# Down products of a shared expert: from row chunk by row chunk to feature tile by feature tile

## The chip, the cores and the metric

The kernel runs on one core of a Trainium2 chip. The metric is the time of one execution on the device in microseconds (us), as the median of several runs. The traces show one execution each, with the engines TensorE (PE; its weight loads are PEld), VectorE (DVE), ScalarE (ACT), GpSimd (POOL) and SyncE (SP, which only issues DMAs here).

## The reference

Input is x of 2 x 2048 rows by 256 features. It is layer-normalised to xn. The output is x + attention(xn) + moe(xn):

```python
xn = layernorm(x)
# attention: 16 heads of 128, blocks with decay, silu on q, k, v, rms norm, sigmoid gate, output product
# moe: 64 experts, top 4 by router logits, plus 2 shared experts that every row passes:
sg = silu(einsum('nd,sdh->nsh', xn, swg))      # S=2, h=256: 512 gate features
su = einsum('nd,sdh->nsh', xn, swu)            # 512 up features
shared = einsum('nsh,shd->nd', sg * su, swd)   # down product, 512 -> 256
```

The change touches the last line only, in the order of its work.

## The kernel before

The kernel has two phases. The **first phase** takes the 4096 rows in NSB = 8 groups of 512 rows (SB), each of CH = 4 row chunks of 128 rows. For each group it normalises the rows, turns them (features onto partitions), computes the router's logits and the choice of experts, and does the whole shared expert. The **second phase** takes 128 steps (16 heads by 8 groups) of attention, and between them scatters rows to the chosen experts, runs these, and adds up. It begins on TensorE right behind the last group of the first phase. Groups, tiles and chunks are counted from 0 in all that follows; a group's window goes from its first logits matmul to that of the next, in the order PE, PEld, DVE, ACT, POOL with the number of instructions in brackets. Each engine runs its own instruction list in the order written; semaphores (`x.wait_ge(sem, n)`, `.then_inc(sem, 1)`) are the only ties between the lists.

Every fp32 product is made of three passes over high and low parts (high by high, high by low, low by high), with operands of type fp32r.

In group g TensorE does in this order:

1. `logits`: 16 small matmuls (L1318), which need `xf` of the group.
2. gate and up products: for each of FT = 4 feature tiles of 128 features 12 matmuls of 512 columns (L1334 to L1336). Tile ft writes bank 4 and 5 (even ft) or 0 and 1 (odd ft); it waits for `sh_ready` of the tile two before.
3. down products: 4 row chunks x 4 feature tiles x 3 passes = 48 matmuls of 256 columns (L1345 to L1347), into bank 6 (chunks 0, 1) and bank 7 (chunks 2, 3). In between stands `rows_T(g + 1)`, 8 transposes (L1304) that turn the next group's rows into banks 0 and 1. It waits for `xn_ready` (the next group's normalised rows, from GpSimd) and for `sh_ready` of all four tiles (banks 0 and 1 free).

Between 2 and 3, each feature tile goes through a chain on two other engines: ACT silu of the gate bank (`ssg`, L705), DVE times the up bank (`sh`, L950), ACT cast to the high part (`shh`, L711), DVE subtract for the low part (`shl`, L955, which counts up `shl_ready`). In the trace `sh` and `ssg` of odd tiles go by the name xf, whose buffer they share.

Other work of a group in the same lists:

- DVE: routing (maximum, top 8, one-hot `oh` L976), and behind `sh` of tile 0 the statistics of the next group's rows (L899 to L905). GpSimd then computes `rs` and four `xn` tiles (L580), which raise `xn_ready`.
- SP: once `xn_ready` of the next group has come, it stores these rows, stores up to three pieces of the split expert down weights (four DMAs for each, L409), and then loads the next up to three pieces (L403).
- ACT: `high_down(0)`, the first cast of a loaded piece (L718), stands in ACT's list between the high part of tile 0 and the silu of tile 1; in groups 1 to 6 there is at least one piece. So silu of tile 1 (and all of the chain behind it) waits for that load.
- ACT also issues a 2 MB zero fill for each group (L670), copies the turned rows out of banks 0 and 1 (`xh` L679, `xf` L681; DVE then makes `xl`, L912) and copies banks 6 and 7 to `res` (L739) when `down_mm` says so.

Of the kernel before, what the change touches and what calls it, by code (L numbers as in the profile page):

```python
# [14 lines left out]
P = 128  # L15
B, N, D = 2, 2048, 256
T = B * N
KD = D // P
# [3 lines left out]
CH = SB // P  # L22
# [5 lines left out]
FT = S * HS // P  # L28
# [34 lines left out]
def lightning_moe(nc, x, slope, wqkv, wgate, wout, norm_w, router_w, router_bias,  # L63
# [12 lines left out]
    with top:  # L76
        def sem(name):
            return top.enter_context(nc.semaphore(name))
# [55 lines left out]
        with ExitStack() as st:  # L134
# [4 lines left out]
            swh = sb("swh", [P, SW], F32R)  # L139
            swl = sb("swl", [P, SW], F32R)  # L140
# [37 lines left out]
            shh = sb("shh", [P, FT, SB], F32R)  # L178
            shl = sb("shl", [P, FT, SB], F32R)
# [76 lines left out]
        shl_ready = sem("shl_ready")  # L256
        down_mm = sem("down_mm")
# [99 lines left out]
        def tok(b):  # L357
            return slice(b * SB, (b + 1) * SB)
# [938 lines left out]
        def _(pe):  # L1297
            def rows_T(g):
                pe.wait_ge(xn_ready, CH * (g + 1))
                pe.wait_ge(xl_ready, KD * g)  # L1300
                pe.wait_ge(sh_ready, FT * g)
                for k in range(KD):
                    for c in range(CH):
                        mm = pe.transpose(bank[k][:, c * P:(c + 1) * P], xn[:, c, k * P:(k + 1) * P], ident[:])  # L1304
                mm.then_inc(xT_mm, 1)
# [6 lines left out]
            def group(g, more):  # L1312
                pe.wait_ge(xf_ready, KD * (g + 1))
                pe.wait_ge(mask_ready, g)
                pe.wait_ge(lc_ready, CH * g)
                for c in range(CH):
                    for k in range(KD):
                        mm = pe.matmul(bank[2][:, c * E:(c + 1) * E], xf[:, k, c * P:(c + 1) * P], rw[:, k, :],  # L1318
                                       start=(k == 0), stop=(k == KD - 1))
                mm.then_inc(logits_mm, 1)  # L1320
                pe.wait_ge(swl_ready, 1)
                pe.wait_ge(xl_ready, KD * (g + 1))
                for ft in range(FT):
                    j = g * FT + ft
                    if ft >= 2:
                        pe.wait_ge(sh_ready, j - 1)
                    elif ft == 1:
                        pe.wait_ge(sh_ready, FT * g)
                    for i in range(2):
                        dst = bank[GU[ft % 2][i]][:]  # L1330
                        for k in range(KD):
                            c0 = (i * KD + k) * 512 + ft * P
                            lh, ll = swh[:, c0:c0 + P], swl[:, c0:c0 + P]
                            pe.matmul(dst, lh, xh[:, k, tok(g)], start=(k == 0), stop=False)  # L1334
                            pe.matmul(dst, lh, xl[:, k, tok(g)], start=False, stop=False)
                            mm = pe.matmul(dst, ll, xh[:, k, tok(g)], start=False, stop=(k == KD - 1))  # L1336
                    mm.then_inc(sgu_mm, 1)

                def down(c, fts):
                    dst = bank[6 + c // 2][:, (c % 2) * D:(c % 2 + 1) * D]  # L1340
                    for ft in fts:
                        c0 = 2 * KD * 512 + ft * D
                        rh, rl = swh[:, c0:c0 + D], swl[:, c0:c0 + D]
                        lh, ll = shh[:, ft, c * P:(c + 1) * P], shl[:, ft, c * P:(c + 1) * P]
                        pe.matmul(dst, lh, rh, start=(ft == 0), stop=False)  # L1345
                        pe.matmul(dst, lh, rl, start=False, stop=False)
                        mm = pe.matmul(dst, ll, rh, start=False, stop=(ft == FT - 1))  # L1347
                    return mm


                pe.wait_ge(swl_ready, 2)
                pe.wait_ge(part_ready, 2 * g)
                pe.wait_ge(shl_ready, FT * g + FT - 1)
                for c in range(0, CH, 2):
                    down(c, range(FT - 1))
                if more:
                    rows_T(g + 1)
                pe.wait_ge(shl_ready, FT * (g + 1))
                for c in range(0, CH, 2):
                    down(c, range(FT - 1, FT))  # L1360
                    down(c + 1, range(FT)).then_inc(down_mm, 1)

            for g in range(NSB - 1):
                group(g, True)
            group(NSB - 1, False)

            def project(dst, h, which, b):
# [263 lines left out]
```

## Time and profile before

| | |
|---|---|
| median of 3 runs | 1710.22 us (1708.69 to 1722.5) |
| the profiled execution, its own time | 1713.04 us |
| its span, first to last instruction | 1711.3 us |
| granted TensorE clock over the span | 0.997 of full |
| PE busy | 1672.8 us (98%) |
| DVE / ACT / POOL busy | 1294.0 / 800.5 / 688.0 us |
| DMA | 345.40 MB, mean 202 GB/s |

The own time is 1.7 us over the span: what lies before the first and behind the last instruction. Matmul rows of a trace overlap: each row's duration holds the pass through the array, so the cost of one in a row of many is the distance between two starts.

### The profile page before, as it was taken

The page shows a single profiled execution, that of the slowest core. Times are in us where ns is not written, and L with a number is a line of the kernel's source. Part 1 is how long each engine was busy: PE and PEld are TensorE (multiplying, and loading weights), DVE is VectorE, ACT ScalarE, POOL GpSimd, SP SyncE. Part 2 cuts the span into 40 slices and gives each one's busy share as a digit, 9 for nine tenths or more (in the row PEclk, how much of TensorE's full clock was granted, in tenths as well). Part 3 has the DMA queues.
Part 4 walks back from the last instruction along what each step waited for, and adds up shares of the span by engine and source line. Part 5 has one row for each costly group of instructions (what it writes and reads, how often), then busy time and mean ns, then how long its engine had stood idle before and what let it go on. Part 6 is the DMA issues. An engine that isn't in the chain of part 4 may idle for free.

```text
span 1711.3 us, 34882 instructions
## 1 busy us (share of the span) xinstructions
PE 1672.8 (98%) x11747; PEld 1539.9 (90%) x11747; DVE 1294.0 (76%) x2595; ACT 800.5 (47%) x1491; POOL 688.0 (40%) x922
## 2 busy tenths in 40 slices
PE   6999999999999999999999999999999999999998
PEld 5888899999998999999989999998999999999998
DVE  6766577888876777777767777777888888887676
ACT  4444443434344555555555555554434343434432
POOL 2333026566555554555545555543333323230011
PEclk9999999999999999999999999999999999999999
DMA  7898544344448999999999999995444444451234
GB/s 234 245 280 263 211 169 152 123 152 133 149 140 249 284 282 296 270 296 276 279 274 269 288 290 282 288 267 161 128 146 130 139 130 144 125 155 56 87 100 135
DMA packets 295727, 345.40 MB, mean 202 GB/s; under 512 B 39680, under 2 KB 239360, under 8 KB 295552
## 3 DMA queue, kind: packets, MB, share of 16 engines
q1 hardware_dynamic: 215488, 179.54, 35.6%
q0 software_dynamic: 41472, 113.30, 22.2%
q10 hardware_dynamic: 38592, 50.34, 8.2%
q8 instruction: 96, 1.57, 0.4%
q14 instruction: 79, 0.65, 0.1%
HBM read 190.19 MB, written 152.85 MB: 200 GB/s over the span
## 4 chain that ended last, share of the span: by engine, by line
PE 88%; issue 5%; POOL 3%; DVE 2%; DMA 1%; SPq 1%; ACT 1%; DVEq 0%; POOLq 0%; ACTq 0%
PE bank L1393 7%; PE bank L1394 7%; PE bank L1392 7%; PE bank L1374 7%; PE bank L1372 7%; PE bank L1373 7%; PE bank L1435 7%; PE bank L1418 7%; PE bank L1438 6%; PE bank L1426 6%; PE bank L1459 5%; PE bank L1448 3%; PE bank L1450 3%; PE bank L1449 3%; POOL xn L580 2%
## 5 line engine op out<-in xcount | busy, mean ns | idle before, releaser
L1393 PE MATMUL bank<-wl,xh 128*128 128x256 f32 x1024 | 289.2, 282 | 0.0
L1394 PE MATMUL bank<-wh,xl 128*128 128x256 f32 x1024 | 289.1, 282 | 0.0
L1392 PE MATMUL bank<-wh,xh 128*128 128x256 f32 x1024 | 289.0, 282 | 0.0
L638 POOL DMA_DIRECT2D xsT<-rows_turned x384 | 211.9, 559 | 137.1 <-DMA rows_turned<-xz 74.3
L769 ACT ACTIVATE kv<-bank 128x512 f32<-128x512 f32 x256 | 153.1, 598 | 207.8 <-PE bank L1394 204.6
L660 POOL DMA_INDIRECT yk<-slot_y,pos x128 | 131.6, 1028 | 253.5 <-DVE xr L1116 170.2
L1372 PE MATMUL bank<-xh,wh 128*128 128x512 f32 x512 | 208.8, 408 | 0.0
L1374 PE MATMUL bank<-xh,wl 128*128 128x512 f32 x512 | 202.4, 395 | 0.0
L1373 PE MATMUL bank<-xl,wh 128*128 128x512 f32 x512 | 201.8, 394 | 0.0
L1392 PEld LDWEIGHTS bank<-wh,xh 128*128 128x128 f32 x1024 | 193.5, 189 | 3.3
L1435 PE MATMUL bank<-sm,kv 128*128 128x128 f32 x1024 | 194.7, 277 | 1.2 <-DVE sm L1136 1.2
L1393 PEld LDWEIGHTS bank<-wl,xh 128*128 128x128 f32 x1024 | 192.9, 188 | 3.1
L1394 PEld LDWEIGHTS bank<-wh,xl 128*128 128x128 f32 x1024 | 192.9, 188 | 0.0
L776 ACT ACTIVATE qT<-bank 128x512 f32<-128x512 f32 x128 | 76.5, 598 | 246.1 <-PE bank L1374 208.4
L1438 PE MATMUL bank<-qp,state 128*128 128x128 f32 x960 | 186.4, 276 | 0.0
L1156 DVE STREAM_TRANSPOSE kz<-kv 128x512 f32<-128x512 f32 x127 | 90.3, 711 | 113.2 <-issue 109.6
L1435 PEld LDWEIGHTS bank<-sm,kv 128*128 128x128 f32 x1024 | 159.4, 193 | 10.9 <-DVE sm L1136 4.6
L1174 DVE SCALAR_TENSOR_TENSOR og<-tg,bank 128x512 f32<-128x512 f32 x128 | 88.0, 687 | 103.0 <-ACT o L797 102.8
L1150 DVE SCALAR_TENSOR_TENSOR state<-state,hc,bank 128x128 f32<-128x128 f32 x448 | 152.0, 339 | 14.5 <-PE bank L1426 1.5
L1190 DVE TENSOR_TENSOR acc<-acc,bank 128x512 f32<-128x512 f32 x238 | 161.8, 680 | 1.0 <-PE bank L1450 1.0
L620 POOL DMA_INDIRECT slot_x<-xs,pos x128 | 135.5, 1058 | 39.8 <-issue 39.5
L1418 PEld LDWEIGHTS bank<-qT,kT 128*128 128x128 f32 x1024 | 132.0, 191 | 21.6 <-issue 12.5
(190 smaller groups left out, 3902.1 us busy)
## 6 DMA issues: line engine op xcount, KB each, us to landing
keys_turned<-kz SPq DMA_DIRECT2D x127, 256.0 KB, 3.3
kT_by_group<-keys_turned SPq DMA_DIRECT2D x508, 64.0 KB
slot_x<-zeros ACTq DMA_DIRECT2D x12, 2048.0 KB, 7.7
xs<-slot_x POOLq DMA_DIRECT2D x96, 256.0 KB, 5.0
we<-wexp_in SPq DMA_DIRECT2D x192, 128.0 KB, 4.2
wd<-expert_down_split SPq DMA_DIRECT2D x192, 128.0 KB, 4.0
rows_turned<-xz POOLq DMA_DIRECT2D x96, 256.0 KB, 4.2
xsT<-rows_turned POOLq DMA_DIRECT2D x384, 64.0 KB, 4.0
```

The source lines that it names most:

```text
L638: pool.dma_start(xsT[q % 2][b * TB:(b + 1) * TB, :, :, :].rearrange("p a k j -> p a (k j)"), xz_back[q % 4, b]).then_inc(xsT_loaded[q % 2] ...
L769: act.activation(kv[i % 2][:, 2 * half:2 * half + 2, :].rearrange("p c n -> p (c n)"), bank[half][:], ACT.Silu).then_inc((k_silu, v_silu)[ ...
L1190: dve.tensor_tensor(a, a, src, ALU.add).then_inc(acc_added, 1)
L1372: pe.matmul(dst, lh, rh, start=(k == 0), stop=False)
L1373: pe.matmul(dst, lh, rl, start=False, stop=False)
L1374: mm = pe.matmul(dst, ll, rh, start=False, stop=(k == KD - 1))
L1392: pe.matmul(dst, lh, rh, start=(k == 0), stop=False)
L1393: pe.matmul(dst, lh, rl, start=False, stop=False)
L1394: mm = pe.matmul(dst, ll, rh, start=False, stop=(k == KD - 1))
L1418: mm = pe.matmul(bank[2][:, ch[c]], kT[:, c, :, :].rearrange("p a j -> p (a j)"), qT[:, ch[c]], start=True, stop=True)
L1435: mm = pe.matmul(bank[4][:, ch[c]], kv[j % 2][:, c, HD:2 * HD], sm[:, ch[c]], start=True, stop=empty)
L1438: mm = pe.matmul(bank[4][:, ch[c]], state[j % 2][:, c, :], qp[j % 2][:, ch[c]], start=False, stop=True)
```

## The change

`down` now does one feature tile of one chunk. The loop over feature tiles is outside and that over all four chunks inside. Each tile has its own wait for its `shl`. The transposes of the next group stand between tile 1 and tile 2: ahead of them 24 down matmuls instead of 18, behind them 24 instead of 30. Each bank's accumulation is opened by one start flag (first matmul of tile 0 of the bank's first chunk), since two chunks of one bank are now in progress at once. `down_mm` is raised behind the sixth and the last matmul of tile 3. The number of matmuls, transposes and casts is the same.

```diff
-                def down(c, fts):
+                def down(c, ft):
                     dst = bank[6 + c // 2][:, (c % 2) * D:(c % 2 + 1) * D]
-                    for ft in fts:
-                        c0 = 2 * KD * 512 + ft * D
-                        rh, rl = swh[:, c0:c0 + D], swl[:, c0:c0 + D]
-                        lh, ll = shh[:, ft, c * P:(c + 1) * P], shl[:, ft, c * P:(c + 1) * P]
-                        pe.matmul(dst, lh, rh, start=(ft == 0), stop=False)
-                        pe.matmul(dst, lh, rl, start=False, stop=False)
-                        mm = pe.matmul(dst, ll, rh, start=False, stop=(ft == FT - 1))
-                    return mm
-
+                    c0 = 2 * KD * 512 + ft * D
+                    rh, rl = swh[:, c0:c0 + D], swl[:, c0:c0 + D]
+                    lh, ll = shh[:, ft, c * P:(c + 1) * P], shl[:, ft, c * P:(c + 1) * P]
+                    pe.matmul(dst, lh, rh, start=(ft == 0 and c % 2 == 0), stop=False)
+                    pe.matmul(dst, lh, rl, start=False, stop=False)
+                    return pe.matmul(dst, ll, rh, start=False, stop=(ft == FT - 1 and c % 2 == 1))
 
                 pe.wait_ge(swl_ready, 2)
                 pe.wait_ge(part_ready, 2 * g)
-                pe.wait_ge(shl_ready, FT * g + FT - 1)
-                for c in range(0, CH, 2):
-                    down(c, range(FT - 1))
-                if more:
-                    rows_T(g + 1)
-                pe.wait_ge(shl_ready, FT * (g + 1))
-                for c in range(0, CH, 2):
-                    down(c, range(FT - 1, FT))
-                    down(c + 1, range(FT)).then_inc(down_mm, 1)
+                for ft in range(FT):
+                    if more and ft == FT // 2:
+                        rows_T(g + 1)
+                    pe.wait_ge(shl_ready, FT * g + ft + 1)
+                    for c in range(CH):
+                        mm = down(c, ft)
+                        if ft == FT - 1 and c % 2:
+                            mm.then_inc(down_mm, 1)
```

## Rows read from the trace of the kernel before

**Rows 1.** The page's head and its first part, the engines' busy time.

```profile
span 1711.3 us, 34882 instructions
PE 1672.8 (98%) x11747; PEld 1539.9 (90%) x11747; DVE 1294.0 (76%) x2595; ACT 800.5 (47%) x1491; POOL 688.0 (40%) x922
```

**Rows 2.** Windows, groups 1 to 3; stretch, us, busy by engine, clock, DMA share, GB/s.

```profile
40.63:61.65 21.02, 19.73 (x123) 17.22 (x122) 14.75 (x42) 10.33 (x22) 7.76 (x5) 1.00 0.63 207
61.65:82.83 21.18, 19.68 (x122) 17.17 (x121) 14.91 (x44) 10.33 (x22) 7.97 (x5) 1.00 0.93 279
82.83:106.42 23.59, 21.24 (x122) 18.72 (x121) 15.17 (x44) 10.21 (x22) 7.05 (x5) 0.93 0.98 283
...
192.00:400.00 208.00, 205.81 (x1501) 187.96 (x1500) 161.98 (x290) 85.03 (x140) 95.75 (x100) 1.00 0.49 163
```

**Rows 3.** Waits from 19 to 192 us: engine, line, releaser: us, times, longest.

```profile
PE bank L1345 <- DVE shl L955: 10.4, 8, 2.4
...
ACT sraw L718 <- DMA sraw<-wdown_in: 2.0, 3, 1.2
```

**Rows 4.** Timeline of TensorE in group 1: start us, duration us, instruction.

```profile
53.42 0.40 PE L1336 MATMUL bank<-xh,swl 128*128 128x512 f32 x1
55.10 0.36 PE L1345 MATMUL bank<-swh,shh 128*128 128x256 f32 x1 [1.29 <-DVE shl L955]
55.30 0.28 PE L1346 MATMUL bank<-swl,shh 128*128 128x256 f32 x1
...
57.24 1.03 PE L1304 MATMUL bank<-ident,xn 128*128 128x128 f32 x8
58.03 0.36 PE L1345 MATMUL bank<-swh,shh 128*128 128x256 f32 x1
...
61.65 1.90 PE L1318 MATMUL bank<-rw,xf 128*128 128x64 f32 x16
```

**Rows 5.** Timeline of the other engines in group 1.

```profile
50.14 6.72 POOL L580 TENSOR_SCALAR xn<-xin,mv,rs 128x256 f32<-128x256 f32 x4 [0.20 <-POOL rs L571]
...
51.58 0.68 DVE L955 TENSOR_TENSOR shl<-xf,shh 128x512 fp32r<-128x512 f32 x1
...
54.22 0.74 DVE L955 TENSOR_TENSOR shl<-sh,shh 128x512 fp32r<-128x512 f32 x1 [0.42 <-ACT shh L711]
...
55.69 0.67 DVE L950 TENSOR_TENSOR xf<-xf,bank 128x512 f32<-128x512 f32 x1
57.05 0.69 DVE L955 TENSOR_TENSOR shl<-xf,shh 128x512 fp32r<-128x512 f32 x1 [0.69 <-ACT shh L711]
...
59.34 1.09 ACT L681 COPY xf<-bank 128x512 f32<-128x512 f32 x2
```

**Rows 6.** Timeline of SP, ACT and DVE from group 1 into group 2.

```profile
57.30 8.63 SPq L409 DMA_DIRECT2D expert_down_split<-sraw  x12
66.04 2.12 SPq L403 DMA_DIRECT2D sraw<-wdown_in  x3
...
68.95 0.62 ACT L718 CAST sraw<-sraw 128x512 fp32r<-128x512 f32 x1 [0.47 <-DMA sraw<-wdown_in]
...
76.92 0.68 DVE L950 TENSOR_TENSOR xf<-xf,bank 128x512 f32<-128x512 f32 x1
```

**Rows 7.** Group 3: timeline of PE and DVE, and one window behind.

```profile
98.37 0.36 PE L1345 MATMUL bank<-swh,shh 128*128 128x256 f32 x1 [2.35 <-DVE shl L955]
98.95 0.68 DVE L950 TENSOR_TENSOR xf<-xf,bank 128x512 f32<-128x512 f32 x1
...
101.00:102.00 1.00, 1.00 (x7) 1.00 (x6) 0.74 (x3) 0.00 (x0) 0.00 (x0) 0.50 1.06 371
```

**Rows 8.** Timeline of TensorE: groups 0 and 7 and the second phase's start.

```profile
34.08 0.36 PE L1345 MATMUL bank<-swh,shh 128*128 128x256 f32 x1 [0.91 <-DVE shl L955]
...
183.25 0.36 PE L1345 MATMUL bank<-swh,shh 128*128 128x256 f32 x1 [0.46 <-DVE shl L955]
...
189.13 0.28 PE L1392 MATMUL bank<-wh,xh 128*128 128x256 f32 x1
```

## The prediction

> **What bounds the kernel now.** I read the head of the page first: TensorE is busy for 1672.8 of 1711.3 us [rows 1], so the time is TensorE's list plus its pauses. The windows say where the pauses are. In the second phase they are small (205.81 busy of 208.00), and nothing there starts by a clock of its own, so a first phase shorter by so much should move all of the second ahead by as much. In the first phase a group takes about 21 us from logits to logits, 1.3 us of it without a matmul; four more groups lie within 0.3 us of these, and group 3 sticks out with 23.59 us and a clock of 0.93 [rows 2]. The list of waits gives the cause: all eight pauses, 10.4 us together, stand before the first down matmul and end with `shl` [rows 3]. The timeline of group 1 shows one of them as lost time. The last gate and up matmul starts at 53.42 and takes 0.24 to the next start, so TensorE could go on at 53.66; it goes on at 55.10, 1.44 us late [rows 4].
>
> **The change, part by part.** Group 1 is worked out in full. Three costs come first, all from rows 4. Eighteen down matmuls take 57.24 - 55.10 = 2.14 us, 0.20 for the first (behind a pause) and 0.115 for each other. The eight transposes take 0.79 us (57.24 to 58.03). The 30 behind them take 61.65 - 58.03 = 3.62 us, again 0.20 for the first and 0.118 for each of 29.
>
> *The wait removed.* Tile 0 now needs only `shl` of tile 0, tile 1 that of tile 1, and the latter is finished at 51.58 + 0.68 = 52.26 [rows 5], 1.4 us before TensorE comes. So the 1.44 us go, and the 24 matmuls of both tiles run from 53.66 to about 56.5 (24 x 0.116 = 2.8).
>
> *What is late next: the transposes.* Before, they came at 57.24 and waited for nothing. Now they would come at 56.5, and two things are needed. `xn` of the next group is finished at 50.14 + 6.72 = 56.86; `sh` of tile 3, which frees banks 0 and 1, at 55.69 + 0.67 = 56.36 [rows 5]. From the end of `shl` to the matmul that it releases I take 0.14 us. This is the step of group 1 itself: tile 2's `shl` ends at 54.22 + 0.74 = 54.96 [rows 5], and the matmul starts at 55.10 [rows 4]. The transposes so start at 57.00, after a new pause of 0.5 us. Behind that wait are queued 24 matmuls and the next group's logits; nobody else is blocked by it before the transposes are done.
>
> *Behind the transposes.* 0.79 us for them and 0.20 + 23 x 0.118 = 2.91 for 24 matmuls: logits at 57.00 + 3.70 = 60.70 instead of 61.65. Tile 2's `shl` was there at 55.10; tile 3's is finished at 57.74 [rows 5], and TensorE needs it at 59.3. The logits need `xf`, copied by ACT to 60.43 before [rows 5]. It hangs on the transposes, which start 0.24 us earlier, so it is done by 60.2, 0.5 us ahead. If that cover were gone (a slower copy), each us would be lost one for one. `down_mm` comes with the sixth and last of the closing matmuls; bank 7's copy still follows the end by the same 0.2 us. Saving in group 1: 0.95 us.
>
> *The same for the others.* Let T be the start of the transposes, counted from the group's logits; the group then lasts T + 3.70. TensorE alone would reach T = 53.66 - 40.63 + 2.8 = 15.8; `xn` allows 16.37 in group 1, `sh` of tile 3 15.87.
>
> - Group 0: the pause shown is 0.91 us [rows 8], 1.06 counted as in group 1 (1.44 lost where the row shows 1.29). No expert piece is in its way, and both inputs of the transposes come before TensorE does, so 1.1 us is saved.
> - Group 2: here the load of the expert pieces comes in. SP begins it after 12 stores of 8.63 us, which begin with `xn` of the group before; ACT gets its piece at 68.95, 12.1 us behind that `xn`, after 0.47 us of idling [rows 6]. This distance is made by DMAs and does not shrink, while group 1 ends 0.95 us earlier. So ACT's silu of tile 1 and the chain behind it are 0.95 us later in group 2. `sh` of tile 3 ended at 77.60, 15.95 behind the logits; now 16.90, plus 0.14: T = 17.04. The group lasts 20.74 instead of 21.18 and saves 0.44.
> - Group 3: `sh` of tile 3 ended at 99.63 [rows 7], 16.80 behind the logits. With the 0.44 of lateness handed on and 0.14, T = 17.38, and the group lasts 21.08 instead of 23.59: 2.5 us saved. 1.5 us of it is clock: from its first down matmul to the logits group 3 took 106.42 - 98.37 = 8.05 us, group 1 took 6.55. Behind its pause of 2.35 us the granted clock was 0.50, the level of 1.2 GHz against 2.4 before [rows 7]. With T = 17.38 the pause is 1.6 us, which is nearer to group 1's 1.44 with its clock of 1.00 [rows 2] than to 2.35.
> - Groups 4, 5 and 6: between group 1's case (`xn` last) and group 2's (the piece last). ACT idled for the load in three groups of six only [rows 3], so some have room for a relative delay, and I take group 1's saving for each: 2.85.
> - Group 7 has no transposes. Its pause of 0.46, 0.6 counted as above, goes. Its 48 matmuls took 189.13 - 183.25 = 5.88 us with two restarts [rows 8]; in one go they take 48 x 0.116 = 5.6, and tile 3's `shl` is there when its turn comes, 4.2 us behind the first. Saving 0.8.
>
> The sum is 1.1 + 0.95 + 0.44 + 2.5 + 2.85 + 0.8 = 8.6 us.
>
> *The waits and the order of banks.* No row prices a satisfied wait alone. The gate and up tiles have such waits, and their starts stand 0.23 to 0.24 apart with or without one. The bound above is the 0.08 us that a first matmul takes more than its neighbours (0.20 against 0.115 [rows 4]): 2 more waits in 8 groups, 1.3 us. The bound below is nothing, since a wait can't speed up its engine. I take nothing. A change of chunk or bank in the middle of the down matmuls costs nothing visible either; from 55.30 to 57.24 there are five changes of tile and one of bank, and the 17 distances average 0.114 us [rows 4].
>
> The Trainium skill (TensorE: Matmul & The Clock Gate, section "A second HAM failure mode: psum-queue depth-cycling") tells of a kernel that cycled through PSUM banks in each iteration, idled briefly between groups of matmuls and had its clock swing. The change does cycle between banks 6 and 7, four times a group. By that rule the result would be that of the clock rival below. Here the clock was 1.00 in the windows of groups 1 and 2, pauses included [rows 2], and only behind the one of 2.35 us was it lower.
>
> The span before was 1711.3, so it comes to 1702.7, and the execution's own time from 1713.04 to 1704.4. The median of the runs lies 2.8 below the profiled one: **1701.6 us**.
>
> **The rivals.**
>
> *A: the new wait takes what the old one gave, in groups 2 to 6.* The load of pieces and the zero fill fill the DMA engines to 0.93 to 0.98 in groups 2 and 3 [rows 2]. If shorter groups only make the pieces land later, T moves up until the old length is back. Left are groups 0, 1 and 7, 2.85 us: 1707.4. For it: ACT idled for this load three times, 2.0 us in all [rows 3]. Against it: groups 1, 4 and 5 have room.
>
> *B: all pauses go.* `xn` would have to be 0.6 us faster than its 6.72 us [rows 5], and the pieces no later than now. The pauses come to 10.4 us [rows 3] and 0.15 more each by the count of group 1, 11.6; with the clock's 1.5 and up to 0.6 for the slower first matmuls it is 13.7 us less, 1696.5. The Trainium skill (SBUF — State Buffer, section "SBUF: two separate sides") says that a GpSimd operation which reads SBUF is held up by a VectorE one with two SBUF inputs; a later chain of `shl` could by that rule move `xn` either way. No row here separates this.
>
> *C, slower: the clock falls.* A group would have up to two pauses, one before tile 3 of gate and up (if `sh` of tile 1 is late by the piece) and one before the transposes. If each sets the clock to 1.2 GHz as in group 3, the price is 1.5 us a time. In groups 1 to 6 that is 12 times, 18 us, less 8.6 gained: 1719.6. It decides from six such falls, where the gain is eaten. Against it: the windows of groups 1 and 2 had none, and the new pauses are shorter, except where the load is late.
>
> **How the numbers follow.** My forecast has 0.67 (own range 1699 to 1705: 0.14 steps, price of waits, groups 4 to 6 each between 0.4 and 1.1), A has 0.17, B 0.09, C 0.05, and 0.02 is for anything else. The range of 8 in 10 takes in the forecast and most of A and B: 1696 to 1710; it also covers that three runs before lay 14 us apart. A measurement of this kernel can tell 1%, 17 us, from no change. That is more than all pauses of the first phase with the clock's part hold, so faster by over 1% has 0.02; slower by over 1% needs more than C as worked out: 0.03; within 1% 0.95.
>
> **What the changed profile would show.** The waits of the first phase: no, or nearly no, pause of L1345 on `shl`, and in its place one of L1304 on `xn` (groups 1, 4, 5) or on `sh` L950 (groups 2, 3), 0.5 to 1.6 us each. The windows: about 20.1 us for group 1, 20.7 for 2, 21.1 for 3 with the clock at 1.00. ACT's pause before L718 longer in group 2, near 1.4 us instead of 0.47. The second phase begins near 180.5 and is as long as before. What would make me wrong: a clock at 0.50 in several groups, a pause of the logits on `xf`, `xn` later than 16.2 us behind the logits, or a second phase that gives the start's gain back.

## The result and the profile after

The changed kernel took 1708.62 us in the median of 20 runs (1702.73 to 1714.5), the kernel before 1714.61 (1707.74 to 1726.01, 20 runs). The ratio is 0.9964, 95% interval 0.9951 to 0.9978: 6.2 us faster, with 3.8 to 8.4 us as the interval. The forecast was 8.6 us. In absolute terms it was 1701.6 us, 7.0 below what was measured. 4.4 us of that are the level of the kernel before: three runs had put it at 1710.22, twenty put it at 1714.61. The other 2.6 us are gain that did not come (the medians differ by 6.0).

The page of the changed kernel, its head and the engines' busy time (beside [rows 1]):

```profile
span 1706.8 us, 34882 instructions
PE 1669.5 (98%) x11747; PEld 1537.9 (90%) x11747; DVE 1293.0 (76%) x2595; ACT 800.7 (47%) x1491; POOL 686.6 (40%) x922
```

Its windows from logits to logits, groups 1 to 3 (beside [rows 2]) and then 4 to 7; columns as there:

```profile
38.17:58.13 19.96, 19.70 (x123) 17.29 (x122) 14.65 (x42) 10.39 (x23) 7.76 (x5) 1.00 0.65 218
58.13:79.03 20.90, 19.80 (x122) 17.10 (x121) 14.86 (x44) 10.16 (x23) 7.37 (x5) 1.00 0.98 299
79.03:99.62 20.59, 19.55 (x122) 17.17 (x121) 15.01 (x44) 10.22 (x23) 7.05 (x5) 1.00 0.96 296
99.62:120.39 20.77, 19.68 (x122) 17.10 (x121) 15.00 (x44) 10.20 (x23) 7.25 (x5) 1.00 0.95 290
120.39:140.96 20.57, 19.69 (x122) 17.29 (x121) 15.07 (x44) 10.34 (x23) 8.37 (x5) 1.00 0.88 261
140.96:160.98 20.02, 19.57 (x122) 17.14 (x121) 13.67 (x42) 9.18 (x21) 7.09 (x5) 1.00 0.98 289
160.98:181.43 20.45, 18.93 (x114) 16.39 (x113) 13.27 (x37) 8.23 (x18) 0.82 (x1) 1.00 0.44 150
```

The granted clock is 1.00 in all of them; group 3's fall is gone. The lengths beside those of before, taken from both traces in the same way, and the forecast:

| group | before | after | gained | forecast |
|---|---|---|---|---|
| 0 | 24.68 | 22.76 | 1.92 | 1.1 |
| 1 | 21.02 | 19.96 | 1.06 | 0.95 |
| 2 | 21.18 | 20.90 | 0.28 | 0.44 |
| 3 | 23.59 | 20.59 | 3.00 | 2.5 |
| 4 | 21.09 | 20.77 | 0.32 | 0.95 |
| 5 | 21.00 | 20.57 | 0.43 | 0.95 |
| 6 | 21.10 | 20.02 | 1.08 | 0.95 |
| 7 | 19.52 | 20.45 | -0.93 | 0.8 |
| sum | 173.18 | 166.02 | 7.16 | 8.6 |

Its waits in the first phase, from 15 to 182 us (beside [rows 3]):

```profile
ACT sraw L718 <- DMA sraw<-wdown_in: 6.8, 5, 1.6
...
PE bank L1304 <- DVE xf L950: 3.7, 4, 1.1
...
ACT wh L753 <- DMA expert_down_split<-sraw: 1.8, 1, 1.8
...
PE bank L1334 <- DVE sh L950: 1.5, 1, 1.5
```

No down matmul waits for `shl` any more; that row, 10.4 us before, has gone. In its place the transposes wait for `sh` of tile 3 (in groups 2, 3, 4 and 6) or for `xn` (in groups 1 and 5; group 1's row is below). ScalarE now idles five times for its expert piece, 6.8 us instead of 2.0. The last two rows are new and lie in group 7.

Group 1 on TensorE and GpSimd (beside [rows 4, 5]), the load of group 2's piece (beside [rows 6]), and group 3's transposes, before which the pause on `shl` has given way (beside [rows 7]):

```profile
47.68 6.72 POOL L580 TENSOR_SCALAR xn<-xin,mv,rs 128x256 f32<-128x256 f32 x4 [0.20 <-POOL rs L571]
...
54.45 1.09 PE L1304 MATMUL bank<-ident,xn 128*128 128x128 f32 x8 [0.27 <-POOL xn L580]
54.84 8.71 SPq L409 DMA_DIRECT2D expert_down_split<-sraw  x12
...
63.66 2.12 SPq L403 DMA_DIRECT2D sraw<-wdown_in  x3
...
66.61 0.62 ACT L718 CAST sraw<-sraw 128x512 fp32r<-128x512 f32 x1 [1.65 <-DMA sraw<-wdown_in]
...
95.98 1.06 PE L1304 MATMUL bank<-ident,xn 128*128 128x128 f32 x8 [1.04 <-DVE xf L950]
```

The transposes of group 1 start 0.05 us behind `xn` (47.68 + 6.72 = 54.40). The piece arrives 12.2 us behind that `xn`, as it did before (12.1), but the group before it is 1.1 us shorter. So ScalarE's idling in group 2 grew from 0.47 to 1.65.

Group 7 and the second phase's first matmul (beside [rows 8]):

```profile
156.97 4.59 SPq L409 DMA_DIRECT2D expert_down_split<-sraw  x4
...
163.57 1.05 ACT L753 CAST wh<-raw 128x1024 fp32r<-128x1024 f32 x1 [1.81 <-DMA expert_down_split<-sraw]
...
164.96 1.23 DVE L1016 TENSOR_TENSOR wl<-raw,wh 128x1024 fp32r<-128x1024 f32 x1 [2.29 <-ACT wh L757]
...
169.32 0.69 DVE L950 TENSOR_TENSOR sh<-ssg,bank 128x512 f32<-128x512 f32 x1
170.06 0.50 PE L1334 MATMUL bank<-xh,swh 128*128 128x512 f32 x1 [1.52 <-DVE sh L950]
...
181.43 0.28 PE L1388 MATMUL bank<-wh,xh 128*128 128x256 f32 x1
```

Read downwards: the last expert piece's four stores are issued from 156.97 on; ScalarE waits 1.81 us for them to land before it may cast head 0's weights; VectorE waits for these casts before it starts the routing of group 7; `sh` of tile 0 is late, and the gate products of tile 2 stand still for 1.52 us. Before the change the gate products of group 7 had no such pause. The same two rows of before:

```profile
164.69 2.84 SPq L409 DMA_DIRECT2D expert_down_split<-sraw  x4
...
170.29 1.05 ACT L753 CAST wh<-raw 128x1024 fp32r<-128x1024 f32 x1
```

The trace also holds the landing of each store. Before, the last one landed at 169.37, 5.1 us behind the end of `xn`, and ScalarE came to the cast 0.9 us later. After the change it landed at 163.55, 7.0 us behind the end of `xn`.

### The profile page after: what moved, and what is told of

Same layout as the page of the kernel before. It is cut to its first block, busy times and chain, and to the rows that moved or that the text cites. A ratio compares the mean times of both kernels' runs of the same rounds, so it can differ in the third digit from the quotient of the medians.

```text
span 1706.8 us, 34882 instructions
## 1 busy us (share of the span) xinstructions
PE 1669.5 (98%) x11747; PEld 1537.9 (90%) x11747; DVE 1293.0 (76%) x2595; ACT 800.7 (47%) x1491; POOL 686.6 (40%) x922
## 4 chain that ended last, share of the span: by engine, by line
PE 88%; issue 6%; POOL 3%; DVE 1%; DMA 1%; SPq 1%; ACT 0%; DVEq 0%; POOLq 0%
PE bank L1389 7%; PE bank L1388 7%; PE bank L1390 7%; PE bank L1370 7%; PE bank L1368 7%; PE bank L1369 7%; PE bank L1431 7%; PE bank L1414 7%; PE bank L1434 6%; PE bank L1422 6%; PE bank L1455 5%; PE bank L1444 3%; PE bank L1446 3%; PE bank L1445 3%; POOL xn L580 3%
## 5 line engine op out<-in xcount | busy, mean ns | idle before, releaser
L1414 PEld LDWEIGHTS bank<-qT,kT 128*128 128x128 f32 x1024 | 133.0, 192 | 20.2 <-issue 10.8
```

Source lines behind the costliest of these rows:

```text
L1414: mm = pe.matmul(bank[2][:, ch[c]], kT[:, c, :, :].rearrange("p a j -> p (a j)"), qT[:, ch[c]], start=True, stop=True)
```

## The experiments

All lengths below run from one group's first logits matmul to the next one's. "First phase" is from the first logits to the first matmul of the second phase: 173.18 us before, 166.02 changed.

**e1: the statistics first.** In VectorE's list, on the changed kernel:

```diff
+                if more:
+                    statistics(g + 1, q + (u + 1) // RING, (u + 1) % RING)
                 dve.wait_ge(logits_mm, g + 1)
...
                 shared(0)
-                if more:
-                    statistics(g + 1, q + (u + 1) // RING, (u + 1) % RING)
```

> The changed kernel with the statistics of the next rows moved in VectorE's list from behind sh of tile 0 to the group's start, ahead of the routing. xn should be ready some 5 us earlier, SP's stores and the piece loads with it. My theory (the new pause is xn or the late expert piece, and in group 7 the last piece's store): the transposes wait for nothing any more, groups 1 to 6 last 19.4 to 19.7 us instead of 20.0 to 20.9, group 7 about 19.0 instead of 20.45, second phase at 174 to 176 instead of 181.4, some 6 us faster than the changed kernel, 12 faster than the kernel before (ratio 0.993). Rival (DMA bandwidth sets the group length, the stores only wait in another place): groups 2 to 5 stay at 20.5 or more, at most 2 us gained.

Measured: 1705.43 us, ratio to before 0.9947 (0.9926 to 0.9967); first phase 162.33. Windows of groups 3, 4, 6 and 7:

```profile
79.13:98.94 19.81, 19.66 (x123) 17.29 (x122) 14.51 (x44) 10.18 (x23) 5.87 (x5) 1.00 0.97 298
98.94:119.24 20.30, 19.64 (x122) 17.25 (x121) 14.63 (x44) 10.20 (x23) 5.87 (x5) 1.00 0.97 303
...
139.19:158.66 19.47, 19.47 (x122) 17.27 (x121) 13.56 (x42) 9.30 (x21) 6.69 (x6) 1.00 0.97 292
158.66:177.92 19.26, 18.94 (x115) 16.40 (x113) 13.14 (x37) 8.20 (x18) 0.00 (x0) 1.00 0.40 144
```

Groups 1, 2 and 6 reach 19.47, in which TensorE is busy throughout. The DMA share is 0.96 to 0.97 in groups 2 and 6, so bandwidth does not set their length. Groups 3 to 5 (19.8 to 20.3) miss the expected 19.7; groups 4 and 5 still wait 0.66 and 0.40 us for `sh` of tile 3. The gain of 3.7 us in the first phase is about six tenths of what I expected; in group 0 the statistics now stand in `sh`'s way (0.75 us) and its time went back to 24.59.

**e2: the piece's cast later.** In ScalarE's list, on the changed kernel:

```diff
                 high(0)
-                high_down(0)
                 gate(1)
                 below_top(g)
                 high(1)
+                high_down(0)
                 high_down(1)
```

> The changed kernel with ScalarE's cast of the group's first expert piece moved behind the silu and high part of tile 1, so that tile 1 no longer waits for the piece's load. My theory: groups 2 to 5 fall from 20.6 to 20.9 to about 20.1, where xn holds the transposes, group 1 stays at 19.96, group 7 stays near 20.4 (its loss is another wait): second phase near 179, 2.5 us faster than the changed kernel. Rival (the load is not what holds sh of tile 3 back, the VectorE list is): groups 2 to 5 keep their length.

Measured: 1705.35 us, ratio 0.9935 (0.9907 to 0.9963); first phase 163.75. Windows of groups 2 and 7, and within group 7 two stretches of 2 us; then TensorE's timeline at the transposes of group 2 and in the gate products of group 7:

```profile
57.86:77.74 19.88, 19.69 (x123) 17.30 (x121) 15.03 (x44) 10.29 (x23) 7.68 (x5) 1.00 0.97 295
...
156.92:179.17 22.25, 20.28 (x114) 17.35 (x113) 13.23 (x37) 8.16 (x18) 0.82 (x1) 0.92 0.42 144
166.00:168.00 2.00, 1.54 (x6) 1.31 (x7) 0.81 (x2) 1.57 (x5) 0.00 (x0) 0.95 0.00 0
168.00:170.00 2.00, 2.00 (x6) 1.52 (x5) 1.97 (x3) 0.93 (x3) 0.00 (x0) 0.50 0.25 94
```

```profile
74.07 1.09 PE L1304 MATMUL bank<-ident,xn 128*128 128x128 f32 x8 [0.19 <-POOL xn L580]
...
166.46 0.51 PE L1334 MATMUL bank<-xh,swh 128*128 128x512 f32 x1 [1.97 <-DVE sh L950]
```

Groups 2 to 5 fall to 19.88 or 19.94, and what is left of their pause is `xn`, 0.2 us. So it was the piece that held `sh` of tile 3 in them. The groups 1 to 6 gained 3.8 us together. Group 7 lost 1.8 of it. It starts 4.1 us earlier than in the changed kernel (156.92 against 160.98), but ScalarE can cast head 0's weights only 3.6 us earlier (159.97 against 163.57), since the last piece's store lands so much earlier and no more. The pause becomes 1.97 us, and the clock falls to 0.50 behind it. I had expected group 7 to stay near 20.4. The second phase begins near 179 as expected only because two misses cancel: groups 1 to 6 gained 3.8 us where I had 2.5, and group 7 lost 1.8.

**e3 and e4: the place of the transposes.** On the changed kernel, in e3 behind 18 down matmuls, in e4 behind 36:

```diff
 e3
-                    if more and ft == FT // 2:
-                        rows_T(g + 1)
                     pe.wait_ge(shl_ready, FT * g + ft + 1)
                     for c in range(CH):
+                        if more and (ft, c) == (1, 2):
+                            rows_T(g + 1)
 e4
-                    if more and ft == FT // 2:
+                    if more and ft == FT - 1:
```

> The changed kernel with the transposes behind 18 down matmuls as before the change, tile order and one wait for each tile kept. My theory: the transposes start at the same moment as in the changed kernel, since xn or sh of tile 3 sets them, after a pause longer by 0.7 us, and six more matmuls stand behind them: groups 1 to 6 longer by 0.7 us each, 4 us in all; second phase at about 185.5. Rival (their place does not matter, only the wait removed does): second phase at 181.5 as in the changed kernel.

> The changed kernel with the transposes behind 36 down matmuls, ahead of tile 3. My theory: no pause ahead of the transposes in group 1 (they start at 17.2 us behind the logits), in groups 2 to 5 hardly any, but now 12 matmuls (1.4 us) do not cover ScalarE's copies of 3.2 us: the logits wait for xf, 1 us or more, and groups last 20.6 to 21.2; second phase at 182 to 184. Rival (a later place is free): groups 1 to 6 at 19.6, second phase at 177.

Measured: e3 1710.48 us, ratio 0.9967 (0.9947 to 0.9987), first phase 168.25; e4 1709.81 us, 0.9971 (0.9946 to 0.9995), first phase 168.47. Timeline of TensorE in e3 at group 1's transposes, and its window of group 1:

```profile
54.64 0.33 PE L1304 MATMUL bank<-ident,xn 128*128 128x128 f32 x1 [0.97 <-POOL xn L580]
...
38.36:58.99 20.63, 19.66 (x123) 17.27 (x121) 14.74 (x42) 10.42 (x23) 7.75 (x5) 1.00 0.65 213
```

In e4 at group 2's logits, and its window of group 1:

```profile
59.34 0.43 PE L1318 MATMUL bank<-rw,xf 128*128 128x64 f32 x2 [0.84 <-ACT xf L681]
...
38.70:59.34 20.64, 19.80 (x121) 17.40 (x121) 14.74 (x41) 10.23 (x23) 7.69 (x5) 1.00 0.65 211
```

In e3 the transposes start 16.28 us behind the logits, exactly as in the changed kernel (54.45 - 38.17), after a pause of 0.97 instead of 0.27; six more matmuls follow, and the group is 0.67 longer. Over groups 1 to 6 it is 2.9 us, not the 4 expected: in the other five the transposes of e3 start up to 0.6 us nearer to the logits than in the changed kernel, and group 7 is 0.8 shorter (a pause of 0.72 on `sh` instead of 1.52). The second phase begins at 183.68, about halfway between my 185.5 and the rival's 181.5. In e4 the transposes wait for nothing, and the 12 matmuls behind them do not cover ScalarE's copies: the logits of group 2 wait 0.84 us for `xf`, and those of all groups from 1 to 7 wait so, 0.8 us in five and 0.5 in two. The middle place is the best of the three. In the first phase it is worth 2.2 us against the old one; the timed ratios, 0.9964, 0.9967 and 0.9971, can't tell these apart.

**e5: the statistics first, without the change.** e1's edit on the kernel before.

> The kernel before with the statistics moved to the group's start, alone. My theory (before the change a group was held by shl of tile 2, which xn does not feed, so earlier xn is worth little without the new order): groups 1, 4, 5 stay at 21.0, only the lateness of the pieces goes in groups 2, 3 and 6, and with it group 3's long pause and clock fall (23.6 to 21.0); first phase 170 us from the first logits instead of 173.2. Rival (the statistics' place is worth its 3 to 4 us by itself): groups at 20.4 or less, first phase under 167.

Measured: 1711.58 us, ratio 0.9967 (0.9948 to 0.9987); first phase 168.59. Its window of group 2 and its wait on `shl` in the first phase:

```profile
60.77:81.50 20.73, 19.73 (x122) 17.22 (x121) 14.75 (x44) 10.32 (x22) 5.87 (x5) 1.00 0.92 287
...
PE bank L1345 <- DVE shl L955: 7.0, 8, 1.0
```

The old order keeps a pause of 1.00 us in six groups, 0.28 less than before: with the statistics gone from behind `sh` of tile 0, VectorE can come to the rest of the chain earlier (this reading was not tested by itself). Group 3 is as long as the others and no clock fall is left. I had expected 170, so the edit alone is worth 4.6 us, more than my theory and less than the rival gave it. In the groups 1 to 6 it leaves 20.7 us where the changed kernel with the same edit has 19.5 to 20.3.

**e6, e7 and e8: the holds taken away one after the other.** e6 is the changed kernel with e2's edit and with e1's from group 1 on. e7 is the changed kernel with the wait for the last piece and the splits of head 0's weights moved into the end of group 7:

```diff
 ACT, ahead of group 7
-            pieces_stored(act)
-            split_high_in(0)
-            split_high_out(0)
 ACT, in group(g, more), behind high(3)
+                else:
+                    pieces_stored(act)
+                    split_high_in(0)
+                    split_high_out(0)
 DVE, the same: from ahead of group 7 to behind shared_low(3)
+                if not more:
+                    scale_out(0)
+                    split_low_in(0)
+                    split_low_out(0)
```

e8 has all three.

> The changed kernel with both moves: statistics first (from group 1 on, group 0 as it was) and the first piece's cast behind tile 1. My theory: no wait is left ahead of the transposes, groups 1 to 6 all at 19.47, the floor that two of these groups showed with the statistics first; group 7 at 19.3 to 19.6; first phase 159 to 161 us from the first logits. Rival (the DMA engines are the next bound): some groups stay at 19.9 or more, with a wait on a piece.

> The changed kernel with the wait for the last expert piece and the splits of head 0's weights moved from ahead of group 7 into its end, behind the high and low parts of tile 3. My theory (the 0.9 us that group 7 lost, and the 0.8 it did not gain, come from ScalarE waiting for the last piece's store ahead of the group, which makes sh of tile 0 late): group 7 falls from 20.45 to 18.7, nothing else moves; first phase 164.2 us instead of 166.0. Rival (VectorE's list in group 7 is what is late): 20 us or more.

> All three moves on top of the change. My theory: groups 1 to 6 at 19.47, group 7 at 18.7, first phase 158 to 160 us from the first logits, 6 to 8 us less than the changed kernel; over all 1701 to 1703 in the median where the kernel before has 1715.7 (ratio 0.992). Rival (the second phase takes back what the first gives): first phase as said, but the span's second part over 1526 us and the ratio at 0.996.

Measured: e6 1702.69 us, ratio 0.9911 (0.9877 to 0.9945), first phase 159.29; e7 1703.84, 0.9938 (0.9918 to 0.9959), first phase 164.32; e8 1698.53, 0.9899 (0.9876 to 0.9922), first phase 158.56. Windows of e6 (group 2), e7 (group 7) and e8 (groups 3 and 7), one fence each:

```profile
57.59:77.06 19.47, 19.47 (x122) 17.27 (x121) 14.63 (x44) 10.29 (x23) 5.87 (x5) 1.00 0.95 293
```

```profile
161.10:179.78 18.68, 18.68 (x114) 16.48 (x113) 13.06 (x36) 8.33 (x18) 0.82 (x1) 1.00 0.47 161
```

```profile
77.71:97.19 19.48, 19.48 (x123) 17.28 (x122) 14.64 (x44) 10.30 (x23) 5.87 (x5) 1.00 0.93 297
155.61:174.29 18.68, 18.68 (x115) 16.48 (x114) 12.93 (x36) 8.29 (x18) 0.73 (x1) 1.00 0.42 152
```

e6 has 19.47 or 19.48 in all of groups 1 to 6, and its group 7 (19.84) still pauses 1.1 us on `sh`. e7 takes group 7 from 20.45 to 18.68 as expected and nothing else moves beyond 0.3 us; its timed gain over the changed kernel is not resolved by itself. In e8, from 19 us to the second phase's first matmul, TensorE has no wait left. It is the best kernel of this study, 1.0% faster than the kernel before. Its median lies 2.5 us under the 1701 to 1703 that I had expected; the first phase is within the expected 158 to 160, so the surplus lies outside it.

**Four repeats of the profile.** Each kernel was profiled twice more.

> The kernel before, profiled once more. My theory: groups 1, 2, 4, 5 and 6 as in the first profile within 0.1 us; group 3's long pause (2.35 us, a late piece) and its fall of the clock need not come again, which is worth up to 2.6 us of the 7.2 that the first phase gained; the second phase varies by some us without the change. Rival: 23.6 us in group 3 again, second phase at 1522.

> The changed kernel, profiled once more. My theory: first phase at 166 us from the first logits within 0.5, second phase anywhere from 1520 to 1530. Rival (the earlier start costs the second phase 3 us each time): 1525 again.

> As the first repeat of the kernel before: a third look at group 0, group 3 and the second phase.

> As the first repeat of the changed kernel: a third look at group 0, group 3 and the second phase.

| | first phase | group 3 | longest other of 1 to 6 | second phase to the end |
|---|---|---|---|---|
| before | 173.18 | 23.59 | 21.18 | 1522.2 |
| before (r1) | 172.82 | 23.56 | 21.47 | 1520.0 |
| before (r3) | 173.99 | 20.90 | 23.74 | 1520.0 |
| changed | 166.02 | 20.59 | 20.90 | 1525.4 |
| changed (r2) | 165.74 | 20.58 | 21.22 | 1527.0 |
| changed (r4) | 165.61 | 20.55 | 21.32 | 1521.9 |

The third profile of the kernel before has the clock fall in two groups, 2 and 4, and not in 3. Their windows:

```profile
60.12:83.36 23.24, 21.36 (x122) 18.86 (x121) 14.93 (x44) 10.21 (x22) 8.35 (x5) 0.93 0.97 276
104.26:128.00 23.74, 21.34 (x122) 18.64 (x121) 15.01 (x44) 10.20 (x22) 7.23 (x5) 0.93 0.90 268
```

So a fall comes in each of three profiles of the kernel before, in one or two groups, and in none of three of the changed one. I had thought it possible that the fall was one of a kind; it is not. The repeats themselves were single executions of 1710.18, 1709.99, 1711.27 and 1704.72 us. The first phase gains 173.33 - 165.79 = 7.5 us in the means. The second part reads 1520.0 to 1522.2 before and 1521.9 to 1527.0 changed, 4.0 us longer in the means. Over all profiles of this study, with the change it is 1520.2 (e1) to 1527.0, without it 1520.0 to 1530.0 (e5).

The traces show what this spread is made of. TensorE's waits in the second phase, first before, then changed; the lines are the score products (L1418, L1414) and the experts' first products (L1459, L1455):

```profile
PE bank L1418 <- issue: 5.3, 6, 2.3
PE bank L1459 <- issue: 2.9, 4, 2.0
```

```profile
PE bank L1455 <- issue: 7.4, 7, 2.5
PE bank L1414 <- issue: 4.6, 3, 3.2
```

With a third row of 1.0 to 1.7 us, TensorE's pauses there come to 9.4, 10.0 and 10.4 us in the three profiles before and to 13.0, 14.0 and 13.0 us in the three of the changed kernel. Falls of the clock to 0.50 cost 3.4, 1.7 and 0 us before, 3.4, 3.4 and 0 changed (half of the time spent at 0.50). With both taken off, the second part is 1508.4 to 1509.7 us in thirteen of the fourteen profiles (1507.7 in e5, which has 15.5 us of pauses and 6.8 of clock). So the spread is pauses and clock. In the first profile of the changed kernel all seven pauses before the experts' products end 0.1 us behind the landing of a load of expert weights (`wd<-expert_down_split`), and the longest one before the scores ends behind a copy of ScalarE that had waited 4.13 us for the DMA of the turned keys.

All eleven profiles in which the second phase begins earlier than in the kernel before (by 4 us or more) have more of these pauses than its three have, 10.8 to 15.5 us. e5, without the change, has the most, and e4, with it, the fewest. No run moves the start alone, so that the earlier start makes them is likely and not shown.

## Why the prediction was right or wrong

- **The wait removed: right.** All eight pauses on `shl` went, and no tile's own wait ever held TensorE.
- **What is late next: right in kind and nearly in size.** Group 1's transposes started 16.28 us behind the logits where I had 16.37. The step of 0.14 us from a result to the work it releases was 0.05 here. e3 shows that the transposes' start is set by their inputs, and e4 that the cover behind them is needed, 3.2 us of it, as worked out.
- **The load that doesn't shrink: right as a mechanism.** Group 2 kept 12.2 us from `xn` to the piece (12.1 forecast), and T was 17.26 against 17.04. e2 settles that it was the piece, since moving only its cast brought groups 2 to 5 down to where `xn` holds them.
- **Groups 4 to 6: mis-sized.** I took group 1's saving for each, 2.85 us, since ScalarE had idled in only three groups of six. They gave 1.83. Their room was less than the lateness handed on by shorter groups: ScalarE idled for the piece in all of groups 2 to 6. In group 5 it was `xn` that came last, for its four tiles took 7.34 us instead of 6.73; it ended 16.85 us behind the logits, later than the 16.2 that I had named as a sign of being wrong. The bound below, group 2's case, was the nearer row for 4 and 5 (0.32 and 0.43 against 0.44).
- **Group 7: wrong, and the step of the gain that failed.** "Its pause of 0.46, 0.6 counted as above, goes. ... Saving 0.8": the pause went, but the group became 0.93 longer, 1.7 us from the forecast. I had followed only the instructions within the group. What stands ahead of it in the lists of ScalarE and VectorE waits for the last piece's store, which is tied to `xn` and the DMAs and not to TensorE. In the trace of before ScalarE shows no idle time ahead of these casts, and I read that as no tie; it was 0.9 us of slack. e7 moves that wait and gets back 1.77 us. The tie is like that of group 2, which I didn't carry over, but the shorter groups are only part of it: `xn` ended 5.4 us ahead of group 7's logits before and 4.5 after (3.8 in the repeats), which uses up the slack and, in the repeats, 0.6 us more. The rest is that the last store landed 7.0 us behind `xn` instead of 5.1 (6.5 and 6.0 in the repeats, 5.1 and 5.3 in those of before). Why it took longer, no run separates.
- **Group 0: 0.8 us more than forecast.** 0.8 of its 1.9 us are the start: after the first logits before, 12 gate products stood 0.42 us apart until they went at 0.23; after, 8 did. The repeats give 24.2 and 23.6 before, 22.8 and 22.3 after, so part of it is chance. The prediction counts four more groups near 21 us; there are three (4, 5 and 6), for group 0 lasts 24.68 and group 7 19.52.
- **Group 3 and the clock: right.** It gained 3.0 us (2.5 forecast), with the clock at 1.00. Rival C did not come about: no group in three profiles of the changed kernel has a fall. Its first kind of pause did come, in the repeats, ahead of tile 3 of gate and up (0.31, 0.58 and 0.17 us), and no fall with it. With a longer pause the fall is real: e2 has one in group 7. The passage of the Trainium skill on PSUM bank cycling (TensorE: Matmul & The Clock Gate, "A second HAM failure mode: psum-queue depth-cycling") has no counterpart in the first phase here. The changed kernel cycles between the banks with pauses of up to 1.63 us, at a clock of 1.00. e8 changes banks just as often, and its groups of 19.48 us hold 19.48 us of matmuls at a clock of 1.00.
- **Rival A** was in between: groups 2, 4 and 5 did keep most of their old length, but mostly because of where the piece's cast stood, and not for bandwidth, since e6 runs group 2 in 19.47 at a DMA share of 0.95.
- **Rival B**, all pauses gone, is what e8 reached by three more edits: 14.6 us less in the first phase, where I had 13.7.
- **The second phase: a term put at nothing, with a reason that doesn't hold.** I had written that "nothing there starts by a clock of its own" and that it would be "as long as before". Its products do wait for loads, as the rows of the repeats show. In the means of three profiles TensorE's pauses there grew by 3.4 us and the whole part by 4.0. Nothing in the prediction priced this, though a second phase that gives the gain back stood among its signs of being wrong.
- **The total.** 7.2 us of 8.6 came in the first phase of the first profile (7.5 in the means of three). Timed it is 6.2 (3.8 to 8.4), which holds 7.5. By the medians the second phase gives back 1 us or so, by the profiles more; how much of that is the change's doing stays open. That the first phase came so near the forecast is partly luck: groups 0 and 3 gave 1.3 us more than forecast, groups 4 to 7 gave 2.75 less.
- **The absolute time: the largest miss, in its base.** "The median of the runs lies 2.8 below the profiled one": over twenty runs it lies 1.6 above (1714.61 against 1713.04). I had set the sum against a median of three runs, and that term makes 4.4 of the 7.0 us.

## What to carry to other kernels

When a wait is removed in a loop, list every event that is tied to something other than the engine made faster (a store that follows a producer, a load behind it), and carry the shift through to the last iteration and the code behind the loop: each such event comes relatively later with every iteration that got shorter. A wait that the profile before doesn't show may have been met with little to spare, 0.9 us here, and the distance to a store or a load is not fixed either (5.1 us became 7.0). Before a base is taken from a few runs, look at how far apart these lie: here it was 14 us. Three small moves in the lists of the other engines (a producer into an idle stretch, a cast and a split behind the work that TensorE waits for) were worth another 7.5 us of the first phase, as much as the change itself.

## What the runs showed of the hardware

- The clock. In the first phase, pauses of TensorE of 1.88, 2.33, 2.35 and 2.40 us ahead of the down products (1.88 and 2.40 in r3, 2.33 in r1) were each followed by a stretch at a granted clock of 0.50, one of 1.97 us in the gate products (e2) too; those of 1.75 us and less were not. The length of a pause does not settle it: in the second phase pauses of 3.02 us (e3, ahead of 524 us) and of 2.48 and 2.50 us (the second repeat of the changed kernel, ahead of 644 and 873 us) had no fall behind them, and one of 2.48 us (changed, ahead of 875 us) had. A fall made its group 2.1 to 2.8 us longer than its neighbours; in group 3 of the first profile 1.1 of the 2.6 is the longer pause itself (2.35 against 1.28), the rest the half clock.
- GpSimd beside VectorE. With the statistics first, `rs` and the four `xn` tiles took 5.87 us of GpSimd in group 1 where they took 7.76 (7.1 to 8.4 in groups 2 to 6 of the changed kernel), the same instructions beside other work of VectorE. The Trainium skill (SBUF — State Buffer, section "SBUF: two separate sides") says that a VectorE operation with two SBUF inputs keeps a GpSimd one that reads SBUF out for its whole length. In their old place the tiles ran beside the `shl` subtractions and those of the piece, which have two such inputs, in the new one beside the reading of PSUM and the top 8. The trace agrees in the main: in group 1 before, three of the four tiles took 1.65, 2.10 and 1.79 us, in e1 each took 1.23. The other one took 1.22 although `shl` of tile 2 ran beside it, which stays unexplained.
- DMA issues. SP took 8.1 to 9.7 us to issue twelve stores of 128 KB in the first profiles of both kernels, and 10.4 to 12.5 us with the statistics first (e1, e5, e6). In group 1 before, these issues were 8.6 of the 12.1 us between `xn` and the next piece. Whether full DMA engines slow the issue down, no run separates.
